# Turning a norm by halves of its tokens, with a first piece of feed-forward work between the halves

## The reference, cut to what matters

```
x = x + L0_xattn(layernorm(x), ctx)       # 32 heads of 128
x = x + L0_ffn(layernorm(x))              # silu(x w1 + b) * (x w2 + b), then w3
x = x + L1_xattn(layernorm(x), ctx)       # 16 heads of 96
x = x + L1_ffn(layernorm(x))              # x W_base + b, plus 8 LoRA experts weighted by sparsemax(x W_router)
x = x + L2_xattn(layernorm(x), ctx)       # 32 heads of 128
x = x + L2_ffn(layernorm(x))              # router scores, top 16 of 64, low-rank experts
x = x + L3_xattn(layernorm(x), ctx)
x = x + L3_ffn(layernorm(x))              # int8 rows with outlier columns
```

## Time and profile before

| what | value |
|---|---|
| runs shown | 1898.87, 1899.39, 1901.48 us; median 1899.39 |
| the profiled execution | 1895.06 us, of which the span is 1893.3 |
| TensorE busy | 1755.8 us, 93% of the span |
| VectorE busy | 1428.1 us, 75% |
| ScalarE busy | 1048.9 us, 55% |
| GpSimd busy | 882.5 us, 47% |
| mean granted TensorE clock | 0.974 of full speed |

### The profile page before, as it was taken

How to read it: one execution, slowest core, us unless ns; L and a number is a source line. 1 busy time by engine, 2 the same in 40 slices (tenths; PEclk the granted TensorE clock), 3 DMA queues, 4 the chain that set the end, 5 groups by cost and what they waited for, 6 DMA issues and landing times.

```text
span 1893.3 us, 28955 instructions
## 1 busy us (share of the span) xinstructions
PE 1755.8 (93%) x9892; PEld 1421.6 (75%) x9892; DVE 1428.1 (75%) x3036; ACT 1048.9 (55%) x1999; POOL 882.5 (47%) x863
## 2 busy tenths in 40 slices
PE   6899999999897999989899999999989999998988
PEld 4677777777676887767688888888867788776755
DVE  6777887878767887766678777778764587786898
ACT  5766667666225565631556556556641387775333
POOL 6766776664633232044344444343346531232762
PEclk9999999999999999999999999999998999998998
DMA  5656656555517988762578778879762100120110
GB/s 185 145 101 144 134 115 142 117 125 112 131 25 142 209 189 174 140 134 73 110 152 196 149 170 173 172 156 194 150 142 101 53 1 23 46 91 29 67 45 23
DMA packets 524177, 226.13 MB, mean 119 GB/s; under 512 B 493696, under 2 KB 503168, under 8 KB 516736
## 3 DMA queue, kind: packets, MB, share of 16 engines
q1 hardware_dynamic: 524032, 224.28, 53.9%
HBM read 97.08 MB, written 5.24 MB: 54 GB/s over the span
## 4 chain that ended last, share of the span: by engine, by line
PE 68%; DVE 16%; DMA 4%; POOL 3%; ACT 3%; issue 3%; SPq 2%; DVEq 0%; POOLq 0%; ACTq 0%
PE ps_t L339 9%; PE ps_t L340 8%; PE ps_t L341 8%; PE ps_s L339 8%; PE ps_s L340 7%; PE ps_s L341 7%; PE ps_o L339 4%; PE ps_o L340 3%; PE ps_o L341 3%; PE ps_o L1887 3%; PE ps_t L1918 3%; PE ps_s L1873 2%; ACT ps_s L1250 2%; DVE nmax L1280 2%; DVE ps_s L1277 1%
## 5 line engine op out<-in xcount | busy, mean ns | idle before, releaser
L1250 ACT ACTIVATE ps_s<-ps_s,nmax 128x768 f32<-128x768 f32 (+1 forms) x320 | 252.6, 789 | 345.9 <-DVE nmax L1280 243.1
L1223 ACT ACTIVATE l_ab<-ps_s,rinv 128x768 f16<-128x768 f32 (+1 forms) x320 | 260.5, 814 | 69.0 <-DVE rinv L1325 54.1
L1318 DVE SCALAR_TENSOR_TENSOR l_ab<-ps_s,rinv,l_ab 128x768 f16<-128x768 f32 (+1 forms) x320 | 289.0, 903 | 2.5 <-ACT l_ab L1223 1.9
L1280 DVE TENSOR_REDUCE nmax<-ps_s 128x1 f32<-128x768 f32 x192 | 183.5, 956 | 124.9 <-PE ps_s L341 124.4
L339 PE MATMUL ps_o<-l_pt,l_v 128*128 128x256 f16 (+1 forms) x832 | 232.8, 280 | 20.2 <-DMA l_v<-l_vab 8.6
L340 PE MATMUL ps_o<-l_pt,l_v 128*128 128x256 f16 (+1 forms) x832 | 231.5, 278 | 0.0
L341 PE MATMUL ps_o<-l_pt,l_v 128*128 128x256 f16 (+1 forms) x832 | 231.5, 278 | 0.0
L339 PE MATMUL ps_s<-l_k_hi,l_q_hi 128*128 128x512 f32 (+3 forms) x512 | 186.3, 364 | 25.1 <-DVE l_ab L1318 21.4
L377 POOL TENSOR_TENSOR wo_hi<-raw_big,one 128x512 fp32r<-128x512 f32 (+2 forms) x100 | 102.5, 1025 | 209.7 <-PE ps_t L341 127.1
L340 PE MATMUL ps_s<-l_k_lo,l_q_hi 128*128 128x512 f32 (+3 forms) x512 | 179.6, 351 | 0.0
L341 PE MATMUL ps_s<-l_k_hi,l_q_lo 128*128 128x512 f32 (+3 forms) x512 | 179.0, 350 | 0.0
(11 more groups left out here) (386 smaller groups left out, 4955.3 us busy)
## 6 DMA issues: line engine op xcount, KB each, us to landing
raw_big<-in_l_wq SPq DMA_DIRECT2D x18, 1024.0 KB, 5.6
raw_big<-in_l_wo SPq DMA_DIRECT2D x18, 1024.0 KB, 5.8
w_raw<-in_f_w SPq DMA_DIRECT2D x32, 256.0 KB, 3.5
raw_big<-in_f_w SPq DMA_DIRECT2D x7, 1024.0 KB, 4.8
raw_kv<-in_l_wkv SPq DMA_DIRECT2D x12, 512.0 KB, 6.5
l_pt<-l_ab SPq DMA_TRANSPOSE x320, 3.7
raw_f<-in_f_w SPq DMA_DIRECT2D x4, 1024.0 KB, 4.8
w_nat<-in_f_w1n SPq DMA_DIRECT2D x16, 256.0 KB, 3.9
```

The source lines that it names most:

```text
L1223: e.activation(sp.ab[:, (k - 1) % 3, 0, :], self.scores_out(k - 1), ACT.Copy, scale=rinv[:, i:i + 1]).then_inc(s_pa, 1)
L1250: e.activation(self.scores_out(k), self.scores_out(k), ACT.Exp, bias=nmax[:, i:i + 1], scale=-1.0 if l.rope else 1.0, accum_out=rsum[:, i: ...
L1280: e.tensor_reduce(nmax[:, i:i + 1], o, AX.X, ALU.max, negate=True).then_inc(s_max, 1)
L1318: e.scalar_tensor_tensor(out=b, in0=self.scores_out(t), scalar=rinv[:, i:i + 1], in1=a, op0=ALU.mult, op1=ALU.subtract).then_inc(s_pb, 1)
```

## The change

For norms 1, 3 and 5 the four banks are shared out in another way. A bank now holds two slices of one half: the banks `ring[0]` and `ring[1]` hold slices 0, 1 and 2, 3 of the first 256 tokens, `ring[2]` and a bank of `ps_t` the same of the last 256. `g_full` is counted up when the two transposes of an odd slice and an odd token tile are through, so that ACT and DVE can take the first half before the second is turned. Each still takes four operations of 128x512 elements per norm, now shaped 128x2x256. In DVE's list the two of the first half stand between `veps` and the scaling of the second half. In PE's list a function `early` stands between the halves: for f0 and f2 the first product for the first 256 tokens, for f1 three of the four slices of token tile 0. Nothing else is added or left out. Norm 7 is left as it was, apart from the way it is written.

```diff
@@ Norm.dve
                     self.dve_stats(e, link, 1)
+                    if self.i == 7:
+                        self.dve_scale(e, 1)
+                        f3_norm_dve(e, link)
+                        return
+                    self.half_lo(e, 0)
                     self.dve_scale(e, 1)
-                    if self.i == 7:
-                        f3_norm_dve(e, link)
-                    else:
-                        turn_dve(e, self.c.g, self.c.hi, xT, self.banks)
+                    self.half_lo(e, 1)
                     return
@@ Norm
+            def half_lo(self, e, half):
+                for p in range(2):
+                    lo_dve(e, *self.half_planes(half, p)[1::-1], self.half_bank(half, p), self.c.hi + 2 * half + p)
+
+            def half_planes(self, half, p):
+                return [a[:, 2 * p:2 * p + 2, half * SQ:(half + 1) * SQ] for a in xT]
+
+            def half_bank(self, half, p):
+
+                return self.banks[2 * half + p].rearrange("p (d t) -> p d t", d=2)
+
-            def pe(self, e):
+            def pe(self, e, early=None):
+                if self.halves and self.i != 7:
+                    for t in range(TT):
+                        half = t // 2
+                        e.wait_ge(s_xn, TT * self.i + t + 1)
+                        for d in range(DK):
+                            mm = e.transpose(self.half_bank(half, d // 2)[:, d % 2, t % 2 * P:t % 2 * P + P],
+                                             xn[:, t, d * P:(d + 1) * P], ident[:, :])
+                            if t % 2 and d % 2:
+                                mm.then_inc(g_full, 1)
+                        if t == 1:
+                            early(e)
+                    return
@@ Norm.act
+                elif self.halves:
+                    for half in range(2):
+                        for p in range(2):
+                            hi_act(e, self.half_planes(half, p)[0], self.half_bank(half, p), self.c.g + 2 * half + p)
+        def half_turned(e, c, half, d):
+
+            e.wait_ge(g_free, c.g - 4 + 2 * half + d // 2 + 1)
@@ token_gemm
+                    if t == 0 and k < begun:
+                        continue
+                    if c is c1 and n == 0 and t % 2 == 0:
+                        half_turned(e, c, t // 2, k)
@@ f0
+        def f0_half(e, half):
+            o = ring_of(0, c0)
+            for d in range(DK):
+                half_turned(e, c0, half, d)
+                mm = passes(e, o[:, half * SQ:(half + 1) * SQ], planes(W["q"], slice(None), d, slice(0, P)),
+                            planes(xT, slice(None), d, slice(half * SQ, (half + 1) * SQ)), d == 0, d == DK - 1)
+            return mm
+
+        def f0_early(e):
+            e.wait_ge(w_rdy["q"], 8 * c0.q + 8)
+            take_bank(e, 0, c0)
+            f0_half(e, 0)
+
         def f0_pe(e):
+            f0_half(e, 1).then_inc(g_full, 1)
@@ f1
+        def f1_early(e):
+            e.wait_ge(w_rdy["kv"], 8 * (c1.kv + 1))
+            o = take_bank(e, 0, c1)
+            for k in range(DK - 1):
+                half_turned(e, c1, 0, k)
+                passes(e, o[:, 0:256], xT_of(k, 0), planes(W["kv"], slice(None), k, slice(0, 256)), k == 0, False)
@@ f2
+        def f2_half(e, half):
+            for d in range(DK):
+                half_turned(e, c2, half, d)
+                mm = passes(e, ps_t[0][0:64, half * SQ:(half + 1) * SQ], planes(W["kv"], slice(None), d, slice(0, 64)),
+                            planes(xT, slice(None), d, slice(half * SQ, (half + 1) * SQ)), d == 0, d == DK - 1)
+            return mm
+
+        def f2_early(e):
+            e.wait_ge(w_rdy["kv"], 8 * (c2.kv + 1))
+            f2_half(e, 0)
...
-            norms[1].pe(e)
+            norms[1].pe(e, f0_early)
```

More of the change, by code:

```diff
@@ L1371, in take_bank, with token_gemm @@
             return ring[r]
-        def token_gemm(e, n, c, a, b, kts, width=512):
+        def token_gemm(e, n, c, a, b, kts, width=512, begun=0):
             for t in range(TT):
-                o = take_bank(e, n + t, c)
+                o = ring_of(n, c) if t == 0 and begun else take_bank(e, n + t, c)
                 for k in kts:
-                    if c is c1:
-                        turned(e, c, k, n + t)
+                    if t == 0 and k < begun:
+                        continue
+                    if c is c1 and n == 0 and t % 2 == 0:
+                        half_turned(e, c, t // 2, k)
                     mm = passes(e, o[:, 0:width], a(k, t), b(k), k == kts[0], k == kts[-1])
@@ L1439, in f0_pe @@
                     n = 2 * j + (role == "o")
+                    if n == 0:
+                        continue
                     o = take_bank(e, n, c0)
                     for d in range(DK):
-                        turned(e, c0, d, n)
                         mm = passes(e, o, planes(W[role], slice(None), d, slice(j * P, (j + 1) * P)),
@@ L1509, in program @@
         s_f1h = sem("f1_experts_weighted")
+        def f1_early(e):
[4 more added lines that the diff above has]
+                passes(e, o[:, 0:256], xT_of(k, 0), planes(W["kv"], slice(None), k, slice(0, 256)), k == 0, False)
         def f1_pe(e):
-            e.wait_ge(w_rdy["kv"], 8 * (c1.kv + 1))
-            token_gemm(e, 0, c1, xT_of, lambda k: planes(W["kv"], slice(None), k, slice(0, 256)), range(DK), 256)
+            token_gemm(e, 0, c1, xT_of, lambda k: planes(W["kv"], slice(None), k, slice(0, 256)), range(DK), 256, begun=DK - 1)
             e.wait_ge(w_rdy["q"], 8 * (c1.q + 1))
@@ L1580, in f2_pool @@
             split_all(e, "o", c2.o + 1, c2.g + 9)
-        def f2_pe(e):
-            e.wait_ge(w_rdy["kv"], 8 * (c2.kv + 1))
-            for d in range(DK):
-                turned(e, c2, d)
-                mm = passes(e, ps_t[0][0:64, :], planes(W["kv"], slice(None), d, slice(0, 64)),
-                            planes(xT, slice(None), d, slice(None)), d == 0, d == DK - 1)
-            mm.then_inc(s_f2r, 1)
+        def f2_half(e, half):
[7 more added lines that the diff above has]
+            f2_half(e, 0)
+        def f2_pe(e):
+            f2_half(e, 1).then_inc(s_f2r, 1)
             o = take_bank(e, 0, c2)
@@ L2474, in _ @@
             a1.pe(e)
-            norms[3].pe(e)
+            norms[3].pe(e, f1_early)
             f1_pe(e)
@@ L2479, in _ @@
             a2.pe(e)
-            norms[5].pe(e)
+            norms[5].pe(e, f2_early)
             f2_pe(e)
```

## The result

| | us |
|---|---|
| before, median of 22 executions on the same chip | 1896.55 |
| after, median of 22 executions | 1888.01 (1883.76 to 1900.14) |
| ratio after to before | 0.996, 95% interval 0.9948 to 0.9972 |
| forecast | 1895.9, range 1893.0 to 1899.3 |

The change makes the kernel faster, by 0.4% (7.6 us by the ratio), about twice the 3.5 us that were forecast; the time lies outside the range. The profiled execution of the changed kernel was the slowest of its 22, 1900.14 us with a span of 1898.3 and a granted clock of 0.971. Read alone, beside the 1895.06 us of the old profile, it would say that the change costs 5 us. So its rows tell what the instructions do, and not what the change is worth.

What follows compares the result with a forecast made beforehand. The prediction took PE, where it stands still, and DVE, where it alone moves the chain, as the bound. -0.7 - 1.8 - 1.0 = -3.5 us gave 1891.6, plus 4.33 for the runs' median 1895.9 us, range 1893.0 to 1899.3.

Steps and rivals of the forecast that it cites:

- The list on DVE and PE: Per norm: two subtractions directly behind `veps`, scaling 0.55 us later, early piece 0.85 after `veps`; no stop at norm 3.
- Norm 1, -0.7: At norm 1, f0's first exponential comes 0.7 us earlier, with ends at -1.05 and +0.4.
- Norm 3, -1.8: At norm 3, f1's last scores come 1.8 us earlier, with the clock back 5.3 us after PE resumes.
- Norm 5, -1.0: At norm 5, the copy of f2's router scores comes 1.0 us earlier, between 0.2 and 1.35.
- rival D: Early piece and second stop keep PE's clock low beyond the hand-over, into f2's first tiles: +4.0 us, 1903.4; chance 0.07.
- The sum, -3.5: Gains at norms 1, 3 and 5 added: -0.7 - 1.8 - 1.0 = -3.5 us, profiled execution 1895.06 to 1891.6.
- The base: The median of the runs shown lies 4.33 us above the profiled execution; this was taken over, giving 1895.9 us.
- A: Clock back sooner, during the second transposes, as PE's work is unbroken for 4 us: -5.0 us, 1894.4; chance 0.26.
- B: Only f1 gains; the clock stays low over both cut products after a longer second stop: -1.0 us, 1898.4; chance 0.15.
- C: The gain is partly hidden by transfers or POOL in the next attention; half of 3.5 us remains: 1897.6; chance 0.10.
- The range: Whole kernel: 1893.0 us, from A with the spread of the runs, to 1899.3, beyond B; nothing of rival D.

Runs made afterwards that it cites:

- f1_only: Against the kernel before, only norm 3 and f1 are done by halves, norms 1 and 5 as before: 1890.32 us, ratio 0.9982.
- before_busy: The kernel before with 16 idle matmuls of 256 columns added in PE's stop at norms 1, 3 and 5: 1889.63 us, ratio 0.9967.
- early_busy: The changed kernel with 15 idle matmuls at the start of PE's stop, ahead of the early piece, at norms 1, 3 and 5: 1887.71 us, ratio 0.9968.
- after_3: The changed kernel run again without edits, for a third profiled execution: 1887.96 us, ratio 0.9959 to the kernel before.
- after_4: The changed kernel run again without edits, for a fourth profiled execution: 1885.91 us, ratio 0.9952 to the kernel before.
- late_busy_2: Second run of the changed kernel with the early piece behind the second transposes and 22 idle matmuls in the stop before these: 1884.0 us, ratio 0.9956.

## Why the prediction was wrong

The direction was right, and the steps on DVE and PE were found where they were put. The size was about half of what was measured. The step that failed and that the profiles show is the price of the clock at norm 3: it was put at -1.8 us, with the clock back 5.3 us after PE resumes, and it measured -3.1, with the clock back after 3.7 us in one kind of execution and never low in another. Where the rest of the surplus lies was not shown.

- **The list on DVE and PE**: right. Subtractions directly behind `veps`, at their usual length (1.28 for two, so 128x2x256 costs what 128x512 does here), not slowed by POOL's root beside them; the scaling 0.29 later (forecast 0.55: the sum counted a start after the end of `veps` and the full length of the second subtraction, where the first starts at 499.50 inside `veps` and the scaling at 500.69 before the second's end at 500.78); the early piece 0.91 after the start of `veps` (499.42 to 500.33; forecast 1.03); stops of 3.16, 2.44 and 3.16 us (forecast 3.3, 2.6, 3.3); a second stop of 1.0 to 1.2 (forecast 1.35); no stop at norm 3. The forecast of an early piece that holds the second transposes back was right too: they start 3.61 us after the start of `veps` (503.03), 2.03 later than before (498.80 less 497.22).
- **Norm 1, -0.7**: about both ends came true, and not the value between, and the clock was not back within 5.5 us of the early piece in most profiles (0.50 up to 508.90 in the first). In four of six profiles with the new norm the hand-over is 9.47, 0.6 over the 8.88 that I compared with (end: +0.4), in two it is 7.93 and 7.80, 1.0 under it (end: -1.05). And 8.88 is itself one of several: six profiles with the old norm average 9.38 (each single-norm run keeps two old norms). Mean against mean it is -0.45; by time, 1.3 and 2.6 us with intervals that include 0.
- **Norm 3, -1.8**: mis-sized. In five profiles with the new norm it is 9.39 four times and 7.80 once, mean 9.07; in seven with the old one 12.2. That is -3.1, beyond the -2.6 that was the end of the term's range, and f1_only's 3.4 us agree with it; 0.3 of it is the old hand-over, which the first profile showed shorter than the mean. The clock was back 3.7 us after the first matmul (857.75 to 861.48) and in one profile never fell. The prediction held it for certain that the clock would be low, though by its own numbers the clock fell at about 852.9 and PE was to resume at 853.0, a margin of 0.1 us; and it took the return after 5.3 us from another place. This is the step that failed most.
- **Norm 5, -1.0**: 8.76 in the mean of five against 9.34 in seven, -0.6, of which f2 gave back 1.6 us in two of the five when the clock stayed low, the seed of rival D.
- **The sum, -3.5**: measured -6.6 by the means of 51 and 178 executions; by the ratios to the executions of the kernel before on the same chips, 0.9951 to 0.996, it is 7.6 to 9.3. What failed in it is the one price for the clock at each norm, read from one execution of the kernel before and carried over. The three norms by their profiles give -0.45 - 3.1 - 0.6, less what f2 gives back, which is hardly more than the forecast; the profiled executions of the changed kernel are slow ones, and so the rest is only argued, from the clocks. The time at the low level, by the granted clocks, is 92.9 us on average before (178 executions) and 80.6 after (51): 12.3 us less. The forecast's three terms hold 5.45 less (returns at 503.55 for 504.9, 858.3 for 859.75, 1427.15 for 1429.8). Among executions of the kernel before a microsecond more at the low level goes with 0.37 us more time, so the 6.9 us that the sum left out would make 2.5: -3.5 - 2.5 = -6.0. This is an estimate, near the 6.6 and under the 7.6 to 9.3; it was not shown norm by norm. before_busy, where only idle matmuls are added, shows that the clock at these places can be worth about 6 us.
- **The base**: the 4.33 us put on top of the profiled time to meet the median of three runs was mostly the chance of three executions: the median of the 22 on that chip is 1896.55 and not 1899.39. So 2.8 of the 7.9 us between the forecast 1895.9 and 1888.01 are the base.
- **The rivals**: A had the right direction, and its -5.0 was nearest; its mechanism, a clock that is back during the second transposes, shows at norm 1 in two of six profiles and at the end of norm 3's transposes. B's picture, a clock that stays low over both cut products, is what four of six profiles show at norm 1, but norm 3 gained more than B had and its total of -1.0 is out (f1_only alone 0.9982, all three 0.9951 to 0.996). C's total is out too, yet POOL does hide part of a larger gain at norm 6, up to 3.1 us in early_busy. D's mechanism is real, as f2's 53.21 us show, but it strikes in two of the four profiles and costs 1.6 us; it does not explain the 1900.14 us of the slowest execution, whose hand-overs are those of after_3 at 1895.97.
- **The range**: it took the spread of the hand-overs from bounds within one execution. Its lower end should have included a clock that doesn't fall at norm 3 and is back early at the others, which after_4 shows: 7.1 us less than the old mean.

## What to carry to other kernels

Where a stop of PE lets its clock fall, price what stands behind it at both levels and take several profiles: the same instructions differed by 4 us in these hand-overs. A change that turns two short bursts with a stop between into unbroken work can earn more than the stop, as at norm 3: 3.1 us for a second stop of some 0.9. Filling a stop with idle matmuls can earn as much, if they stand where nothing waits for them; put one place too late they made the kernel 10 us slower. Ask also which other engine has no slack where the gain is to arrive: here POOL's memset at norm 6 caps what norm 5 can pass on. The lowest mean here, 1885.4 us, belongs to the early piece behind the transposes with 22 idle matmuls in the stop; against the kernel before on the same chips its ratios are those of the changed kernel.

## What was not expected of the hardware

- One kernel's executions spread over 19 us (1880.67 to 1900.14 for the changed one) with identical instructions; their granted clocks range with them, from 0.983 to 0.971.
- Work did not always bring the clock back or hold it: PE was busy for 8.39 of 8.50 us in late_busy_2 at a mean granted clock of 0.70, and at norm 5 of the changed kernel it stayed at 0.50 for 13.7 us with PE busy for 10.9.
- At norm 3 the clock fell behind a stop of 2.44 us in one execution of the changed kernel, for 3.7 us, and did not fall at all around a stop of 2.59 us in another (granted 1.00 in it and behind it).
- A DVE instruction of 128x4 elements took 3.83 us while POOL's memset ran and 0.73 in the kernel before; in both it ended with the memset.
